# A wait between GpSimd's scaled query product and VectorE's decay scan in a chunked delta-rule attention kernel

## What is computed

```python
q, k, v = (silu(conv4(x @ W)) for W in (Wq, Wk, Wv));  k *= 128 ** -0.5
alpha, beta, g = sigmoid(x @ Wa + ba), sigmoid(x @ Wb + bb), sigmoid(x @ Wg)
err = S @ k_t - v_t                          # S: 128 x 128 state
S = alpha_t * S - beta_t * outer(err, k_t)
o_t = S @ q_t
out = (layernorm(o) * g) @ Wo
```

## Time and profile before

| | us | what it is |
|---|---|---|
| median of three runs | 2385.58 | 2385.12 to 2389.96 |
| profiled execution | 2385.5 | its span, first to last instruction |
| PE busy | 2299.3 | 96% of the span |
| DVE busy | 2051.2 | 86% |
| ACT busy | 1989.9 | 83% |
| POOL busy | 1892.8 | 79% |
| decay scan, L1614, 128 of them | 215.5 | busy time on DVE, mean 1683 ns |
| PE idle before L3174 | 38.9 | of it 37.8 until DVE's L1712 |

### The profile page before, as it was taken

How to read it: one execution, slowest core, us unless ns; L and a number is a source line. 1 busy time by engine, 2 the same in 40 slices (tenths; PEclk the granted TensorE clock), 3 DMA queues, 4 the chain that set the end, 5 groups by cost and what they waited for, 6 DMA issues and landing times.

```text
span 2385.5 us, 65201 instructions
## 1 busy us (share of the span) xinstructions
PE 2299.3 (96%) x25520; PEld 1756.6 (74%) x25520; DVE 2051.2 (86%) x4283; ACT 1989.9 (83%) x3956; POOL 1892.8 (79%) x2063
## 2 busy tenths in 40 slices
PE   5999999999999999999999999999999999999999
PEld 2555777777777777777777777777777777777765
DVE  8789998888888888888999888888888888899654
ACT  3877888888888888888888888888888888889865
POOL 4875788888888888888888888888888888889875
PEclk8999999999999999999999999999999999999999
DMA  5441111111121111111111011101210121111001
GB/s 141 129 144 57 34 33 24 33 33 33 29 63 42 33 30 27 33 33 32 47 50 42 24 33 33 33 24 33 68 38 28 33 53 33 28 33 33 17 28 45
DMA packets 72849, 103.65 MB, mean 43 GB/s; under 512 B 21472, under 2 KB 33760, under 8 KB 72416
## 3 DMA queue, kind: packets, MB, share of 16 engines
q1 hardware_dynamic: 72544, 99.48, 16.0%
HBM read 85.69 MB, written 13.77 MB: 42 GB/s over the span
## 4 chain that ended last, share of the span: by engine, by line
PE 67%; DVE 13%; ACT 7%; issue 2%; POOL 1%; DVEq 0%; ACTq 0%; POOLq 0%
PE bank L3174 21%; DVE a_prod L1614 5%; DVE k_rows L1712 5%; PE bank L3104 4%; PE bank L3145 4%; PE bank L3090 4%; PE bank L3105 4%; PE bank L3244 3%; PE bank L2996 3%; PE bank L3010 3%; PE bank L3008 3%; PE bank L2924 2%; PE bank L2926 2%; PE bank L2925 2%; PE bank L2970 2%
## 5 line engine op out<-in xcount | busy, mean ns | idle before, releaser
L1712 DVE SCALAR_TENSOR_TENSOR k_rows<-bank,k_prm,k_rows 128x509 f32<-128x509 f32 (+2 forms) x1152 | 819.9, 736 | 1.6 <-ACT k_rows L2286 0.2
L3174 PE MATMUL bank<-k_z,k_kqv 128*128 128x512 f16 x2304 | 617.9, 380 | 38.9 <-DVE k_rows L1712 37.8
L2378 ACT ACTIVATE k_wide<-bank 128x512 f16<-128x512 f32 x640 | 378.9, 592 | 64.9 <-PE bank L3010 60.5
L1644 DVE TENSOR_TENSOR k_y<-bank,k_masks 128x256 f16<-128x256 f32 x768 | 305.8, 411 | 97.8 <-PE bank L2996 97.1
L2286 ACT ACTIVATE k_rows<-bank,k_prm 128x512 f32<-128x512 f32 x384 | 300.7, 783 | 69.0 <-PE bank L3174 68.8
L1331 POOL TENSOR_TENSOR k_narrow<-k_narrow,k_rows 128x512 f32<-128x512 f32 x128 | 171.0, 1336 | 157.9 <-ACT k_narrow L2412 157.9
L3174 PEld LDWEIGHTS bank<-k_z,k_kqv 128*128 128x128 f16 x2304 | 178.7, 98 | 147.5 <-DVE k_rows L1712 49.3
L2296 ACT ACTIVATE k_rows<-k_rows 128x512 f32<-128x512 f32 x384 | 220.9, 620 | 68.3 <-DVE k_rows L1712 68.1
L2996 PEld LDWEIGHTS bank<-k_wide 128*128 128x128 f16 x3072 | 180.9, 98 | 100.7 <-ACT k_wide L2361 7.2
L3010 PE MATMUL bank<-k_wide,k_y 128*128 128x64 f16 x3072 | 251.7, 193 | 0.6 <-DVE k_y L1644 0.6
L1232 POOL TENSOR_TENSOR k_wide<-k_solve,k_ident 128x512 f16<-128x512 f32 x128 | 163.2, 1275 | 103.4 <-DVE k_solve L1623 103.0
(11 more groups left out here) (171 smaller groups left out, 6613.3 us busy)
## 6 DMA issues: line engine op xcount, KB each, us to landing
a_decay<-decay_rows SPq DMA_DIRECT2D x128, 258.0 KB, 3.5
k_solve<-cumulative_rows SPq DMA_DIRECT2D x96, 258.0 KB, 3.4
weight_pairs<-k_wide SPq DMA_DIRECT2D x15, 512.0 KB, 2.9
k_kqv<-weight_pairs SPq DMA_DIRECT2D x9, 512.0 KB, 4.9
stream<-in_L_attn_x SPq DMA_DIRECT2D x8, 512.0 KB, 7.6
out<-stream SPq DMA_DIRECT2D x7, 512.0 KB, 2.9
k_rows<-in_L_attn_Wk SPq DMA_DIRECT2D x4, 512.0 KB, 4.8
k_rows<-in_L_attn_Wq SPq DMA_DIRECT2D x4, 512.0 KB, 5.0
```

What stands on the lines that cost most here:

```text
L1644: nc.vector.tensor_tensor(even(y16[:, j], mb), bank[LEV[par]][:, 0:U * C // 2].rearrange("p (u b m) -> p u b m", u=U, m=mb), masks[:, j].r ...
L1712: nc.vector.scalar_tensor_tensor(out=dst[:, d:S], in0=bank[PJ[j % 2]][:, 0:S - d], scalar=prm[:, i, U * (n // B) + j, TAPS - 1 - d:TAPS - ...
L2378: nc.scalar.activation(both, bank[LEV[par]][:, :].rearrange("p (two b m) -> p two b m", two=2, m=mb), ACT.Copy).then_inc(m[f"act_lev{par}" ...
L3174: mm = pe.matmul(bank[PJ[j % 2]][:, :], wt, z16[:, zh, k, cols], start=(x == 0), stop=(x == 5))
```

## The change

GpSimd waits, ahead of `scaled_q(t)`, for the count t + 3 on `dve_scan`, that is until the scan of step t + 2 has ended, in all steps but those of the edges:

```diff
             if t % NC == NC - 1:
                 need(pool, m["pe_o"], t)
+            if not edge(t):
+                pool.wait_ge(m["dve_scan"], t + 3)
             nc.gpsimd.tensor_tensor(qg[:, :, :], qb[:, n % 2, :, c * C:(c + 1) * C], cum[:, :, 1:CX],
                                     ALU.mult).then_inc(m["pool_qg"], 1)
```

## The result

The changed kernel takes 2342.44 us (2341.68 to 2343.31) against 2385.77 for the kernel before; the ratio is 0.9815, with a 95% interval of 0.9801 to 0.9829. The forecast was 2338.5 in a range of 2330 to 2367.

The account below looks back on a forecast made before the run. TensorE was taken to set the pace for most of each step, VectorE's scan for a few microseconds. Gain 48.1 less 1.0 made 47.1: 2385.6 - 47.1 = 2338.5 us, range 2330 to 2367.

Parts of the forecast that it names:

- step (1): VectorE's scans in A and B become short with GpSimd waiting: 28 x 0.76 + 26 x 1.03 = 48.1 us gained.
- A: Steady-loop stretch opened by scan index 3 mod 4, with a long scan; forecast to gain 0.76 us, 28 times.
- B: Steady-loop stretch opened by scan index 0 mod 4, with a long scan; forecast to gain 1.03 us, 26 times.
- (2): GpSimd's wait itself: `scaled_q` starts about 0.07 us after the scan's end, running 1.29 to 2.57 from the scan's start.
- (3): GpSimd's queue behind `scaled_q`: `system16` may start at 3.80; TensorE's `first_inverse` loses 0.04 us per B, 1.0 in 26.
- (4): In C the wait is pure delay, `gated` ending 0.5 us later; costed at nothing, bound 1.4 us.
- C: Steady-loop stretch with a short scan, where `scaled_q` was over before the scan; forecast to stay as before.
- step (5): SyncE's queue: the load of `cum` goes out later, takes 3.5 us, leaving 0.15 us before `scaled_k`.
- (7): GpSimd as the bound: its round in A, 15.62 us, fits A's new length 15.88 with 0.26 to spare.
- the slow load: Rival: loads of `cum` back to back with those of the decays become slow, GpSimd waits; some 2425 us, chance 0.05.
- `system_low` in the way: No-change rival: GpSimd falls back about 1 us, the scan meets `system_low` and stays long; 2386 us, chance 0.07.

## Why the prediction was right, and where its 4 us went

**The cause, step (1): right.** Scans of A and B are short, the stall of TensorE is gone, and the wait moved it nowhere in most steps. B's 1.03 had a row, the stretch where the scan had got in first, and came out as 1.02. A's 0.76 had none: it was A's late start with the 0.10 that B had shown beyond its own, and it came out as 0.76 in every kernel that has the wait there. That it fits to the hundredth is luck; only the bounds, nothing and 0.99, were shown.

**The wait and what is behind it, (2), (3) and (4): right, a little too dear.** `scaled_q` starts 1.39 after A's scan began and 1.30 after B's (1.29 had been forecast), and takes 1.18, not 1.28, so `system16` starts 3.68 into B, not 3.80:

```profile
1329.45 1.18 POOL L1286 TENSOR_TENSOR k_narrow<-k_rows,k_solve 128x512 f32<-128x512 f32 x1 [1.26 <-DVE a_prod L1616]
...
1331.83 1.28 POOL L1232 TENSOR_TENSOR k_wide<-k_solve,k_ident 128x512 f16<-128x512 f32 x1
```

The 1.28 came from a wrong reading: `gated` and `system16` take 1.27 and 1.29 in the earlier trace rows too, where neither idled before, so that time is their own, and `scaled_q` takes 1.18 after an idle 1.26 as well. The 0.04 per B that was set aside for TensorE's `first_inverse` was not lost. In C the delay is real and covered, as the kernel with that wait alone shows.

**The load of `cum`, step (5): the term that was mis-sized.** The landing time was taken from a single stretch, 3.5 us, which left 0.15, and the rest was to go into the idle time before `root`. In the changed kernel the median of A's landings is 3.8 and 10 of 28 take more than 4. GpSimd idles before `scaled_k` 27 times, 14.7 us in all, which the prediction had named as the sign of this step being wrong. That overdraws the margin of (7), 0.26, by a few tenths in some ten A, and `system_low` then meets the scan of the B behind; in two of these B a late load of their own holds up `query_low` besides. It cost 3.65 us in the first trace: 2385.5 - 48.1 + 3.65 = 2341.05, and the span is 2340.9. The trace of before had another price for two such loads close together: in its C the load of `cum` goes out 0.43 us behind that of the decays, and lands after a median of 4.0 us. The two kernels that take this away, by a later reader and by a later second load, are at 2338.87 and 2339.64. The rivals named both pieces, the slow load and `system_low` in the way, but each was priced as a case of all steps; here they work together in a third of the B.

**The time around the span: wrong.** The text put nothing between span and time. Every run with both numbers shows 1.7 us or so, those of the kernel before among them; the changed kernel took 2342.67 with a span of 2340.9. So the execution of before whose span was shown took some 2387.2 us, an estimate, and the median belongs to faster ones. The changed kernel is 3.9 above the forecast; 3.65 for `cum` and 1.7 around the span, less the 1.0 set aside in (3), make 4.35.

These terms hold for the two profiled executions. By medians the gain is 43.3 us in the first comparison and 47.0 in the last one, because the kernel before took 2385.77 there and 2389.17 here while the changed one stayed. So how near the forecast gain of 47.1 came depends on the baseline. Part of what moves it is in the traces: each B whose race the scan wins is worth 1.03, and the kernel with the wait in C alone, which leaves that race open, has four of them in place of two and a span 2.1 shorter. The rest is open.

## What to carry to other kernels

Look for one shape of instruction with two durations, and for what a neighbouring engine does at its start. A wait that only orders two engines can be free or even a gain, if the one that waits has idle time behind it; what has to be counted is everything that is released later by it, and a load that is shifted next to another one should be priced at the landing time it will have there, not at the median of before. Where a margin of tenths decides, move the reader of the load back by one or two places.

## What the runs showed of the hardware

- VectorE's scan with both inputs in SBUF and a GpSimd product with its inputs in SBUF did not run side by side: whichever came second stood still, 0.99 to 1.06 us for the scan where the two began together, 1.0 for the product. A GpSimd fill of the same tile (0.53 us) ran beside the scan at no cost. The Trainium skill, SBUF — State Buffer, "Who interferes with whom", says both, though it does not name the scan: a VectorE instruction with two SBUF inputs contends with a GpSimd instruction that reads SBUF, not with one that only writes it.
- The race for it is decided by hundredths of a microsecond: from the second B on, both instructions begin within 0.01 us of each other in the kernel before, and the scan went first in 1 of 27; with the wait in C alone it was 3 of 27.
- A load of 258 KB that has a second one put out 0.37 us behind it landed after a median of 3.8 us in A; with none behind it until it had landed, after 3.2.
